# Four edits in a graph network on one core: packed words and pairwise one-hots in the counting, a node row in PSUM, late products on GpSimd, divisions on ScalarE

## What is computed

```python
x = x + L0(h)   # attention, 8 heads, exp(clip(leaky(a_src[src] + a_dst[dst]))), summed per src node
x = x + L1(h)   # two mean layers: segment_sum(h[src], dst) / deg @ w_l + b + h @ w_r, relu between
x = x + L2(h)   # msg = h[src] * edge_attr (100000 x 64); mean over dst; concat; @ W.T + b
x = x + L3(h)   # attention with segment max over dst and self loops, mean over heads,
                # layer norm, two-layer net with relu, layer norm
```

## Time and profile before

| | |
|---|---|
| median of 3 runs | 5207.26 us (5205.52 to 5208.05) |
| the profiled execution's own time | 5206.89 us |
| its span | 5205.2 us |
| mean granted TensorE clock | 0.728 of full |
| PE busy | 3125.2 us, 60% |
| PEld busy | 2024.9 us, 39% |
| DVE busy | 3109.6 us, 60% |
| ACT busy | 1812.4 us, 35% |
| POOL busy | 1698.0 us, 33% |
| counting, last to first matmul of line 543 | 102.7 to 525.3 us |
| tile_sum, gathers | 2520 to 3545 us |
| attend3, groups | 3775 to 5009 us |
| finish_layer3 | 5011 to 5205 us |

### The profile page before, as it was taken

How to read it: one execution, slowest core, us unless ns; L and a number is a source line. 1 busy time by engine, 2 the same in 40 slices (tenths; PEclk the granted TensorE clock), 3 DMA queues, 4 the chain that set the end, 5 groups by cost and what they waited for, 6 DMA issues and landing times. The chain is left out here.

```text
span 5205.2 us, 45137 instructions
## 1 busy us (share of the span) xinstructions
PE 3125.2 (60%) x11765; PEld 2024.9 (39%) x11765; DVE 3109.6 (60%) x4761; ACT 1812.4 (35%) x2737; POOL 1698.0 (33%) x1687
## 2 busy tenths in 40 slices
PE   5999799877878777789344333334033433423764
PEld 4999344322222222456233333333022333423642
DVE  6999799999999999310232111112244655646875
ACT  1444799988888888000000000000011111211300
POOL 0000000000000000000577777773777666665200
PEclk7999899999999999899555555555555555555556
DMA  1323677544444443878222422212111111111020
GB/s 31 99 90 101 197 214 213 152 124 115 119 122 120 122 119 96 181 181 183 63 49 52 99 51 51 50 35 30 27 39 34 39 33 32 38 33 29 6 52 28
DMA packets 294100, 448.72 MB, mean 86 GB/s; under 512 B 180002, under 2 KB 183965, under 8 KB 284439
## 3 DMA queue, kind: packets, MB, share of 16 engines
q1 hardware_dynamic: 241577, 390.49, 28.2%
q0 software_dynamic: 52288, 55.34, 5.5%
HBM read 351.39 MB, written 94.23 MB: 86 GB/s over the span
## 5 line engine op out<-in xcount | busy, mean ns | idle before, releaser
L896 PE MATMUL l_sum_ps<-arena,sums 125*65 125x500 f32 (+1 forms) x2600 | 1155.7, 584 | 248.1 <-DVE arena L790 218.7
L1814 POOL DMA_INDIRECT l_rows<-table,tile_src x782 | 770.1, 985 | 351.8 <-issue 222.4
L1225 POOL DMA_INDIRECT l_rows<-hidden_rows,tile_src x782 | 787.5, 1007 | 238.1 <-issue 238.1
L779 DVE SCALAR_TENSOR_TENSOR arena<-arena,far_past 125x750 f32<-125x750 f32 (+1 forms) x800 | 805.3, 1046 | 17.8 <-DMA arena<-score_rows 17.8
L825 ACT ACTIVATE arena<-arena,far_left 125x750 f32<-125x750 f32 (+1 forms) x800 | 716.9, 950 | 166.9 <-DVE arena L779 166.8
L1278 PE MATMUL l_acc_ps<-l_rows,l_hot 128*125 x1612 | 360.9, 413 | 649.2 <-DVE l_rows L1242 635.5
L790 DVE SCALAR_TENSOR_TENSOR arena<-arena,l_turned 125x1500 f32<-125x1500 f32 (+1 forms) x400 | 710.7, 1777 | 49.3 <-ACT arena L830 42.8
L896 PEld LDWEIGHTS l_sum_ps<-arena,sums 125*65 125x65 f32 x2600 | 334.6, 139 | 1003.9 <-issue 544.3
L830 ACT ACTIVATE arena<-arena 125x1500 f32<-125x1500 f32 (+1 forms) x400 | 601.4, 1504 | 0.0
L1278 PEld LDWEIGHTS l_acc_ps<-l_rows,l_hot 128*125 128x125 f32 x1612 | 340.1, 321 | 671.0 <-issue 668.7
L1242 DVE TENSOR_TENSOR l_rows<-l_rows,l_attr 128x512 f32<-128x512 f32 x98 | 68.4, 698 | 814.8 <-DMA l_rows<-hidden_rows,tile_src 814.8
(11 more groups left out here) (464 smaller groups left out, 2938.1 us busy)
## 6 DMA issues: line engine op xcount, KB each, us to landing
l_turned<-turned_counts SPq DMA_DIRECT2D x225, 328.1 KB
arena<-counts SPq DMA_DIRECT2D x17, 2843.8 KB
counts<-arena SPq DMA_DIRECT2D x25, 1421.9 KB
l_turned<-turned_counts SPq DMA_DIRECT2D x75, 382.8 KB
l_attr<-edge_attr_in SPq DMA_DIRECT2D x97, 256.0 KB
arena<-counts SPq DMA_DIRECT2D x75, 328.1 KB
turned_counts<-l_turned SPq DMA_DIRECT2D x75, 328.1 KB
arena<-score_rows SPq DMA_DIRECT2D x24, 732.4 KB
```

Of the source, the lines that this page charges most:

```text
L779: last = v.scalar_tensor_tensor(scores(k)[:, i, :], rows[:, 1, i, :], m.far_past[:, w, h:h + 1], rows[:, 0, i, :], ALU.add, ALU.max)
L896: last = nc.tensor.matmul(sum_ps[0:F + 1, c, 0:hi - lo], h_one[:, w, :], z[k % ZS][:, lo:hi], start=(w == 0), stop=(w == W - 1))
L1225: pool.indirect_dma_start(rows[:, b % RING, t, :], None, m.hidden_rows[:, :], bass.IndirectOffsetOnAxis(ap=m.tile_src[:, k:k + 1], axis=0) ...
L1814: pool.indirect_dma_start(rows[:, t % RING3, :], None, m.table3[:, :], bass.IndirectOffsetOnAxis(ap=m.tile_src[:, t:t + 1], axis=0)).then_ ...
```

## The change

```diff
+ROUNDS = KV // UV
+TURN_ROOM = 128
+LATE = 172
...
+            for i in range(UV):
+                v.memset(slot_place[:, i:i + 1], float(SLOTS ** i))
+            for i in range(UV // AT_LOAD):
+                last = v.memset(turn_place[:, i:i + 1], float(TURN_ROOM ** i))
...
-            own(v.tensor_copy(t.turn[:, :], row[:, 0:KV // AT_LOAD]))
+            own(v.tensor_tensor(turns.rearrange("p (r i) -> p r i", r=ROUNDS), ..., over(turn_place ...), ALU.mult))
+            own(v.tensor_reduce(below[:, 0:ROUNDS], turns.rearrange("p (r i) -> p r i", r=ROUNDS), AX.X, ALU.add))
+            own(v.tensor_copy(t.words[:, 1:2 * ROUNDS:2], below[:, 0:ROUNDS]))
...
-            own(v.tensor_copy(t.slot[:, :], row[:, :]))
+            own(v.tensor_tensor(row ..., row ..., over(slot_place ...), ALU.mult))
+            own(v.tensor_reduce(below[:, 0:ROUNDS], row[:, :].rearrange("p (r i) -> p r i", r=ROUNDS), AX.X, ALU.add))
+            own(v.tensor_copy(t.words[:, 0:2 * ROUNDS:2], below[:, 0:ROUNDS]))
...
-        self.src_hot = hot[:, UV * CW:].rearrange("p (a c i) -> p a i c", a=NARROW // UV, i=UV)
-        self.node_step = s.sb("node_step", [P, P, UV], F16)
+        self.src_hot = hot[:, UV * CW:].rearrange("p (a g c i) -> p a g c i", a=NARROW // UV, g=UV // 2, i=2)
+        self.node_step = s.sb("node_step", [P, P, 2], F16)
...
-            if k % AT_LOAD == 0:
-                slots = self.values(mybir.EngineType.PE, m.fine.slot, k, AT_LOAD, SLOTS - 1)
-            if k % AT_LOAD ** 2 == 0:
-                turns = self.values(mybir.EngineType.PE, m.fine.turn, k // AT_LOAD, ...)
-            if k % AT_LOAD == 0:
-                pe.wait_ge(self.slot_free, turns[k // AT_LOAD % AT_LOAD])
+            i = k % UV
+            if i == 0:
+                slots, turns = self.values(mybir.EngineType.PE, m.fine.words, k // UV * 2, 2, SLOTS ** UV - 1)
+            if i % AT_LOAD == 0:
+                turn = turns if i + AT_LOAD == UV else turns & (TURN_ROOM ** (i // AT_LOAD + 1) - 1)
+                pe.wait_ge(self.slot_free, nc.tensor.snap(turn >> 7 * (i // AT_LOAD)).with_bounds(min_val=1, max_val=V))
+            slot = ((slots >> 2 * i) & (SLOTS - 1)).with_bounds(min_val=0, max_val=SLOTS - 1)
...
# tile_sum
+        row_ps, row_copied = s.ps("row_ps"), s.sem("row_copied")
-                                over(m.node_row[:, :].unsqueeze(1), (TILE, U, P)), ALU.is_equal).then_inc(hot_ready, 1)
+                                over(row_ps[:, 0:P].unsqueeze(1), (TILE, U, P)), ALU.is_equal).then_inc(hot_ready, 1)
+            v.tensor_copy(row_ps[:, 0:P], m.node_row[:, :]).then_inc(row_copied, 1)
...
# attend3
+        def late(g):
+            return g >= LATE and (g < PART * (NP - 1) // STEPS or g % 3 > 0)
...
+            for g in range(LATE, groups):
+                o, n = STEPS * g % HERE, len(steps_of(g))
+                pool.wait_ge(here_ready, STEPS * g // HERE + 1)
+                if late(g):
+                    pool.wait_ge(sums_ready, g - 2)
+                    pool.wait_ge(step_ready, g + 1)
+                    nc.gpsimd.tensor_tensor(hot[g % 3] ..., over(here ...), over(step_att ...), ALU.mult).then_inc(late_hot_ready, 1)
+                if g >= PART * (NP - 1) // STEPS + 4 and n_found < 2 * J:
+                    if n_found == 0:
+                        pool.wait_ge(top_written, 16 * NP)
+                    find(n_found)
+                    n_found += 1
...
# finish_layer3
-            divide(0)
-            divide(1)
-            dve.wait_ge(base_in, 32)
-            own(v.tensor_tensor(y[:, :, :], h[:, :, :], rowwise(bias_att), ALU.add))
...
-                if w + 2 < W:
-                    divide(w + 2)
+                if w == GROUP:
+                    dve.wait_ge(base_in, 16)
+                    dve.wait_ge(vectors_in, 16)
+                    own(v.tensor_tensor(y[:, :, :], h[:, :, :], rowwise(bias_att), ALU.add))
...
+            pool.dma_start(vectors[:, :], io["rows"][3:9, :].rearrange("a n -> (a n)").partition_broadcast(P)).then_inc(vectors_in, 16)
-            sp.dma_start(vectors[:, :], io["rows"][3:9, :].rearrange("a n -> (a n)").partition_broadcast(P)).then_inc(base_in, 16)
...
+            def divide(w):
+                for o in range(w * per, (w + 1) * per):
+                    here = m.acc[:, o, 0:F]
+                    last = nc.scalar.activation(here, here, ACT.Copy, scale=inv[:, o:o + 1])
+                last.then_inc(acc_ready, 1)
+            act.wait_ge(less_ready, 1)
+            divide(0)
...
+            for w in range(1, 2 * GROUP):
+                divide(w)
             for g in range(groups):
+                if g + 2 < groups:
+                    for w in blocks_of(g + 2):
+                        divide(w)
```

More of the change, by code:

```diff
@@ L385, in _ @@
             own(v.tensor_tensor(row[:, :], row[:, :], below[:, :], ALU.add))
-            own(v.tensor_copy(t.slot[:, :], row[:, :]))
+            own(v.tensor_tensor(row[:, :].rearrange("p (r i) -> p r i", r=ROUNDS), row[:, :].rearrange("p (r i) -> p r i", r=ROUNDS),
+                                over(slot_place[:, :].unsqueeze(1), (1, ROUNDS, UV)), ALU.mult))
+            own(v.tensor_reduce(below[:, 0:ROUNDS], row[:, :].rearrange("p (r i) -> p r i", r=ROUNDS), AX.X, ALU.add))
+            own(v.tensor_copy(t.words[:, 0:2 * ROUNDS:2], below[:, 0:ROUNDS]))
             dve.wait_ge(left_ready, 1)
@@ L1759, in part_groups, with hots @@
             return range(PART * p // STEPS, PART * (p + 1) // STEPS if p + 1 < NP else groups)
+        def late(g):
+            return g >= LATE and (g < PART * (NP - 1) // STEPS or g % 3 > 0)
+        def hots(g):
+            by_pool = sum(late(x) for x in range(g + 1))
+            return (late_hot_ready, by_pool) if late(g) else (hot_ready, g + 1 - by_pool)
         @block.sync
@@ L1816, in _, with find @@
                                         ).then_inc(rows_in[t // U % RING], 16)
-            pool.wait_ge(top_written, 16 * NP)
-            for c in range(2 * J):
+            def find(c):
                 pool.indirect_dma_start(found[:, c // J, c % J, :], None, m.reference[:, :],
@@ L1821, in _ @@
                                         ).then_inc(found_in, 16)
+            n_found = 0
+            for g in range(LATE, groups):
[4 more added lines that the diff above has]
+                    pool.wait_ge(step_ready, g + 1)
+                    nc.gpsimd.tensor_tensor(hot[g % 3][:, 0:n, :, :], over(here[:, STEPS * g // HERE % 2, o:o + n, :].unsqueeze(2), (TILE, n, H, J)),
+                                     over(step_att[:, g % AHEAD, 0:n, :].unsqueeze(3), (TILE, n, H, J)), ALU.mult
+                                     ).then_inc(late_hot_ready, 1)
+                if g >= PART * (NP - 1) // STEPS + 4 and n_found < 2 * J:
[3 more added lines that the diff above has]
+                    n_found += 1
+            assert n_found == 2 * J
         @block.vector
@@ L1909, in build @@
             def build(g):
+                o, n = STEPS * g % HERE, len(steps_of(g))
+                if o and late(g):
+                    return
                 if g >= 3:
                     dve.wait_ge(sums_ready, g - 2)
-                o, n = STEPS * g % HERE, len(steps_of(g))
                 if o == 0:
-                    ahead = min(HERE, KJ - STEPS * g)
-                    v.tensor_tensor(here[:, 0:ahead, :], over(m.rel3[:, STEPS * g:STEPS * g + ahead].unsqueeze(2), (TILE, ahead, J)),
+                    block, ahead = STEPS * g // HERE, min(HERE, KJ - STEPS * g)
+                    by_pool = sum(late(x) for x in range(g - HERE // STEPS))
+                    if by_pool:
+                        dve.wait_ge(late_hot_ready, by_pool)
+                    v.tensor_tensor(here[:, block % 2, 0:ahead, :],
+                                    over(m.rel3[:, STEPS * g:STEPS * g + ahead].unsqueeze(2), (TILE, ahead, J)),
                                     over(m.window_iota[:, :].unsqueeze(1), (TILE, ahead, J)), ALU.is_equal).then_inc(here_ready, 1)
                     dve.wait_ge(here_ready, STEPS * g // HERE + 1)
+                if late(g):
+                    return
                 dve.wait_ge(step_ready, g + 1)
-                v.tensor_tensor(hot[g % 3][:, 0:n, :, :], over(here[:, o:o + n, :].unsqueeze(2), (TILE, n, H, J)),
+                v.tensor_tensor(hot[g % 3][:, 0:n, :, :], over(here[:, STEPS * g // HERE % 2, o:o + n, :].unsqueeze(2), (TILE, n, H, J)),
                                 over(step_att[:, g % AHEAD, 0:n, :].unsqueeze(3), (TILE, n, H, J)), ALU.mult).then_inc(hot_ready, 1)
@@ L2002, in sums @@
             def sums(g):
-                pe.wait_ge(hot_ready, g + 1)
+                pe.wait_ge(*hots(g))
                 if g >= 4:
@@ L2114, in _ @@
             own, v = Own(dve, own_sem), nc.vector
-            def divide(w):
-                o = w * per
-                here = m.acc[:, o:o + per, 0:F]
```

(3 more changed lines are left out.)

31 lines of the change are left out of this document (20 added, 11 removed).

## The result

The changed kernel takes 5296.6 us (median of 4, 5289.2 to 5308.2) against 5207.7 (5205.5 to 5210.6): ratio 1.0169, 95% interval 1.0151 to 1.0188. Forecast were 5111, in a range of 5082 to 5172. It is slower by 89 us. Rival 3 had said slower (5257), by 50.

What follows compares the result with a forecast made beforehand. Stages follow each other; the counting was held by the array, with VectorE and TensorE's stream within 20%. Counting -60, tile layer -9, late products -8, end layer -19 sum to -96: 5207 to 5111 us, range 5082 to 5172.

Steps and rivals of the forecast that it cites:

- Rival 3: Counting: TensorE's instruction stream becomes the bound, shift and mask cost as the 166-ns kind, 6.6 us a round, 5257; chance 0.10.
- Counting, the step that failed: Counting, TensorE's stream: shift and mask for each of 24 addresses at 0.142 us a step, 4.5 us a round; counting -60.
- the cheap end: Counting: the longer address operation taken at 64 ns, 0.142 us a step, against 166 ns at the other end.
- Counting, a second step: Counting: with paired one-hots a matmul takes 0.138 us, the array 3.3 us a round; the round falls to 4.7.
- Three limits within 20%: Counting before the change, per round: array 5.2 us, TensorE's instruction stream 4.9, VectorE 4.44; the array is the last.
- The layout's premise: Counting: weights 4 bytes apart load like packed ones (0.136 us), against 0.312 at 24 bytes apart.
- rival 2: Counting: VectorE's narrow one-hot falls to the f32 pace, at most 1.9 us, round up to 5.4, 5165; chance 0.08.
- Mean layer: Tile layer: one-hot input in PSUM frees 20 gathers, the 78 message-product hits stay; -9, from -12 to 0.
- Late products: Late attention groups: products on GpSimd at 1.4 us, groups 0.34 us shorter where no find runs; -8, from -19 to +20.
- rival 4: Late attention stretch: GpSimd's products at 3 us under exclusion, +12 instead of -8, 5131; chance 0.10.
- End layer, start: End layer's start: broadcast off SP's queue, so the weights' write comes earlier; -6, from -3 to -9.
- End layer, loop: End layer's loop: divisions leave VectorE, 19 of them on the path at 0.69 us; -13, from -14 to -5.

Runs made afterwards that it cites:

- end_h: Kernel before with the end layer's changes, node features' load moved behind the seventh weights load, bias add at window 8: ratio 0.9971.
- end_only: Kernel before with the end layer's changes alone (divisions on ScalarE, broadcast on GpSimd's queue, bias add in the loop): ratio 0.9972.
- best_b: Kernel before with pairs, 12-slot reads, node row in PSUM, late products, earlier flags and window numbers, end layer's changes with moved load: ratio 0.9922.

## Why the prediction was wrong

- **Counting, the step that failed.** It said "each of the 24 addresses needs a shift and a mask more" and priced that as a longer fused operation of 64 ns, 0.142 us a step, with 166 ns as the other end. The compiler kept the address at 46 ns and put shift and mask into operations of their own, one pair for a step's two matmuls, at 0.097 us each: a step with its two matmuls is 0.44 us instead of the forecast 0.28 (2 x 0.142), 0.25 before. Rival 3 had the place right (TensorE's stream becomes the bound) and put 6.6 us a round, which the undisturbed rounds take; the reads inside the counts' transfers bring 7.05. But it came to 6.6 by luck: it had one operation of 166 ns per address, and its own sign, register operations over 130 ns, did not show. Its chance of 0.10 was too low: the estimate of the cheap end was the nearest duration in a list, not an argument on what the compiler emits.
- **Counting, a second step.** "The array is out of it", and with it the round was to fall to 4.7: even with the old tables the pairs gave nothing. At 96% busy, the array (5.24) looked like the bound, while the stream at 5.47 was the longer one. My 4.9 for the stream left out the three waits (0.33) and was short by 0.13 on the steps and on the reads. "Three limits within 20%" was right, their order was not.
- **The layout's premise held.** Loads 4 bytes apart take 0.137 us: by the Trainium skill's rule (SBUF — State Buffer, Door 1: The DMA port swizzle), that at least two accesses should fall in a line of 16 bytes, the trace agrees. The narrow one-hot stayed at 0.93, and rival 2 is out.
- **Mean layer.** "At most 20 x 0.5 = 10 come back", with the 78 hits of the message product left as they are. The 20 went, and 29 of the 78 with them: -22. I took the hits as fixed to their operation.
- **Late products.** "The next table read (0.33, hidden under the product until now) comes partly free": nothing came free. It had been hidden under the product, the wait for the own accumulation stands ahead of it, and both together are as long as the product. Both numbers are in the trace of before; I had the read and did not add the wait of 0.32. GpSimd's product takes 1.05 us (1.50 at most), not 1.4, and rival 4 is out. That the Trainium skill's exclusion (SBUF — State Buffer, Who interferes with whom) would bring the edit to zero came out in number, but not by that mechanism: VectorE's products fell from 168.6 to 131.1 us of work over the layer, and the time stayed behind as waits of its own.
- **End layer, start.** "The broadcast leaves SP's queue, so the weights' write no longer waits 8.32 us behind it": 6 us less were forecast, 1.5 came. The issue time of an instruction was taken for its own cost. It was its place behind a load of 3125 rows of 256 bytes: end_h, without that load ahead, starts its first product 15.4 us behind the last accumulation, end_only 23.6.
- **End layer, loop.** The mechanism was right (the divisions leave VectorE: a window takes 2.73 us instead of 3.33), its size was not: 13 forecast, 7.1 measured. By the trace the rest was given back by TensorE's clock: the head matmuls of the fifth group take 5.79 us instead of 4.22. ScalarE's division takes 0.336 us, one every 0.24, and its cover held.

## What to carry to other kernels

Before trading table reads for register arithmetic, count the instructions that the engine's sequencer must issue, at about 0.1 us each from start to start, whatever their duration says, and put that sum beside the array's; an engine that is 96% busy need not be the limit: here the array's 5.24 us a round stood under the stream's 5.47, and making the array faster showed only where the stream had been brought under it. An instruction removed from a chain gains nothing when a wait and a read of its length lie hidden beneath it: read the gap between its neighbours in the place where the instruction is absent. A long issue on a DMA queue belongs to what was issued before it; move that, not the one that waits.

The version to take is best_d: words out, one wide read a round, slot waits on VectorE, pairs, node row in PSUM, late products with the early read, and the end layer with the moved load: 0.9806 of the kernel before, on a chip where before takes 5510 us. On a chip like the prediction's it wasn't timed; an estimate from best_b's 5171 us and the 59.5 us between the two countings is 5111 us, 0.981.

## What the runs showed of the hardware

- A plain register operation of TensorE's sequencer: 36 ns by the trace, 0.097 us to the next instruction. The fused address operation: 46 ns, 0.095 us to the load of its weights, 0.124 to the next address operation.
- A table read of 4 values 0.33 us, of 12 0.85, of 2 0.54; up to 1.6 (4 values), 2.4 (2) and 3.6 (12) when it starts while a 1.6 MB transfer out of SBUF runs. Outside such transfers 211 of 215 lay within 12 ns in the kernel before. VectorE's and ScalarE's reads in the same stretch went up to 2.5 and 1.6 as well.
- While finds follow each other at 1.3 us, the register operations of ScalarE take 0.7 and 1.4 us instead of 0.064 on some chips, and not on others.
- The DMA issued behind a load of 3125 rows of 256 bytes on SP's queue stands 7.2 to 9.4 us, whichever it is; `own_turned` elsewhere took 0.45.
- GpSimd's gathers that begin under a VectorE operation with two SBUF inputs take 0.45 to 0.50 us longer; with one input of the one-hot in PSUM none was held by it, and of 98 such gathers 49 were left, not 78.
- Weights 24 bytes apart load in 0.312 us and let a matmul of 325 columns start every 0.218; 4 bytes apart they load in 0.137. At the lower clock level, 1.2 GHz, such a matmul starts every 0.272 us.
